# State space scan tiles regrouped: 16 states by 8 channels, with dt and dt·u repeated by DMA

## The reference

```
x = layernorm(x + attention(x))            # 32 heads of 8, relative bias, softmax, wo
x = layernorm(x + ssm(ctx_1024, z=x))      # state space layer, below
x = layernorm(x + moe(x))                  # softmax router, top 1 of 4 experts, silu(g)*u
```

```
dt_low, B, C = split(x_proj(u))            # 8, 16 and 16 rows
dt = softplus(dt_proj(dt_low) + bias)      # per channel d
A = -exp(A_log)                            # 256 channels x 16 states
state[d, n] = state[d, n] * exp(dt[d] * A[d, n]) + dt[d] * u[d] * B[n]   # over tokens
y[d] = sum_n state[d, n] * C[n] + D[d] * u[d];   out = y * silu(z)
```

## Time and profile before

| | us |
|---|---|
| median of the runs | 476.77 |
| the profiled execution, its own time | 477.8 |
| its span (first to last instruction) | 476.0 |
| PE busy | 421.8 (89%) |
| DVE busy | 314.9 (66%) |
| POOL busy | 223.6 (47%) |
| ACT busy | 211.2 (44%) |
| chain that ended last, by engine | PE 63%, DVE 19%, POOL 7%, issue 7%, ACT 2%, DMA 1% |

### The profile page before, as it was taken

The page is one execution under the profiler, slowest core; times in us unless marked ns, Lnnn a source line. Parts: engine busy times, 40 slices in busy tenths (PEclk is TensorE's granted clock), DMA queues, the critical chain, the costliest instruction groups (busy, mean ns, idle before and its releaser), DMA issues.

```text
span 476.0 us, 7872 instructions
## 1 busy us (share of the span) xinstructions
PE 421.8 (89%) x2569; PEld 212.5 (45%) x2570; DVE 314.9 (66%) x626; ACT 211.2 (44%) x412; POOL 223.6 (47%) x246
## 2 busy tenths in 40 slices
PE   5989698878788998989989899986999999999993
PEld 3444223323334443444434444353546666666652
DVE  3598667999988878878889687578314433333444
ACT  2557437566545557745577466712022111111220
POOL 2000518787787569976699768800461111111001
PEclk9999766999989999999999999999999999999997
DMA  9789947717157191674414530069220000000000
GB/s 237 102 269 102 304 138 100 130 64 138 45 117 129 46 154 46 140 195 157 150 72 178 179 98 14 1 251 355 85 61 11 12 4 8 11 11 11 11 1 9
DMA packets 39366, 49.36 MB, mean 104 GB/s; under 512 B 4664, under 2 KB 32673, under 8 KB 39334
## 3 DMA queue, kind: packets, MB, share of 16 engines
q1 hardware_dynamic: 36322, 46.65, 38.8%
q0 software_dynamic: 1056, 2.10, 1.5%
q10 hardware_dynamic: 1956, 0.21, 0.4%
HBM read 40.72 MB, written 8.91 MB: 104 GB/s over the span
## 4 chain that ended last, share of the span: by engine, by line
PE 63%; DVE 19%; POOL 7%; issue 7%; ACT 2%; DMA 1%; POOLq 0%; SPq 0%; DVEq 0%; ACTq 0%
PE ps L1180 16%; PE ps L1196 8%; PE ps L881 7%; PE ps L908 5%; DVE arena L1566 5%; PE ps L912 4%; PE ps L954 4%; DVE arena L1499 4%; PE ps L781 3%; DVE arena L1517 3%; POOL arena L653 2%; PE ps L941 2%; PE ps L1188 2%; POOL arena L659 2%; PE ps L794 2%
## 5 line engine op out<-in xcount | busy, mean ns | idle before, releaser
L1366 ACT ACTIVATE arena<-ps 128x512 f32<-128x512 f32 x128 | 76.2, 595 | 90.7 <-PE ps L941 90.5
L1517 DVE TENSOR_REDUCE arena<-ps 128x2 f32<-128x512 f32 x128 | 86.3, 681 | 27.0 <-PE ps L912 23.0
L659 POOL TENSOR_TENSOR arena<-arena 128x512 f32<-128x512 f32 x60 | 76.2, 1270 | 41.6 <-DVE arena L1566 41.5
L653 POOL TENSOR_TENSOR arena<-arena 128x512 f32<-128x512 f32 x64 | 87.0, 1361 | 4.1 <-issue 3.9
L1180 PE MATMUL ps<-arena 128*128 x176 | 77.5, 593 | 0.7 <-ACT arena L1407 0.7
L1566 DVE TENSOR_TENSOR_SCAN arena<-ps,arena 128x512 f32<-128x512 f32 x60 | 72.8, 1214 | 0.5 <-DVE mv L1611 0.2
L881 PE MATMUL ps<-arena,identf 128*128 128x512 f32 x128 | 68.6, 623 | 0.0
L908 PE MATMUL ps<-arena 48*128 48x256 bf16 x256 | 52.1, 285 | 16.1 <-DVE arena L1517 10.9
L1325 ACT ACTIVATE ps<-arena 128x255 f32<-128x255 f32 x128 | 60.4, 473 | 2.4 <-DVEq L1723 2.4
L1834 DVE TENSOR_TENSOR arena<-arena,ps 128x1024 f32<-128x1024 f32 x11 | 13.4, 1222 | 59.8 <-ACT arena L1411 59.8
L729 POOL DMA_INDIRECT out<-rows_s,arena x11 | 10.8, 985 | 88.7 <-DVE rows_s L1863 80.5
(11 more groups left out here) (231 smaller groups left out, 530.5 us busy)
## 6 DMA issues: line engine op xcount, KB each, us to landing
arena<-bc_d SPq DMA_DIRECT2D x32, 512.0 KB, 4.4
arena<-in_L_ffn_Wg SPq DMA_DIRECT2D x8, 512.0 KB, 5.8
arena<-in_L_ffn_Wu SPq DMA_DIRECT2D x8, 512.0 KB, 6.0
arena<-in_L_ffn_Wd SPq DMA_DIRECT2D x4, 1024.0 KB, 11.8
arena<-kp_d SPq DMA_DIRECT2D x8, 384.0 KB, 8.2
arena<-qp_d SPq DMA_DIRECT2D x8, 384.0 KB, 10.4
qp_d<-arena SPq DMA_DIRECT2D x4, 384.0 KB, 8.6
kp_d<-arena SPq DMA_DIRECT2D x4, 384.0 KB, 8.5
```

What stands on the lines that cost most here:

```text
L653: g.tensor_tensor(dBu[m % 3], dtu[:, :, b * SEQ:(b + 1) * SEQ], over_k(bcr[c % BC_RING][:, m % 2, 0, :]), ALU.mult).then_inc(dbu_ready, 1)
L659: g.tensor_tensor(h, h, over_k(bcr[m // 2 % BC_RING][:, m % 2, 1, :]), ALU.mult).then_inc(hc_ready, 1)
L1366: A(prob[2 * (slot % 2) + kt][:, pr * HALF:(pr + 1) * HALF], ps[:, 2 + n % 2, :], ACT.Exp).then_inc(p_ready, 1)
L1517: v.tensor_reduce(negm[b % 2][:, qt, 2 * pair:2 * pair + 2], ps[:, bank, :].rearrange("p (h k) -> p h k", h=2), axis=AX.X, op=ALU.max).the ...
```

## The change

A tile becomes 16 states by 8 channels, for both halves: partition 8 n + c holds state n of channel c of the group `tile_of(m)`. The 16 tiles of a batch are now 16 groups of 8 channels.

- dt and dt·u of a batch are stored to DRAM (`store_dd`, two stores of 256 KB) and, for each tile, 8 partitions of 4 KB are loaded 16 times over (`load_dd`, 512 KB, a ring of four). ScalarE and GpSimd read this tile. B and C need one load of 256 KB a batch (`load_bc`).
- A is laid out anew (`rates`): transposed by TensorE, exponentiated, stored to DRAM and loaded again by ScalarE's own DMA queue, negated.
- `sum_states(b, q)` sums four tiles at once: `pick` (128 x 32) has ones where partition 8 n + c belongs to column 8 q + c, and each of the four matmuls writes another 32 PSUM partitions.
- `softplus(1)` moves ahead of the loop; the chores begin at n = 3 and come after every unit. `keep_warm(9)` goes. `put_max(0, 1)` comes after the release of the loop. `rows_s` lends its memory to `hst`, `bcs`, `pick` and `rates`, and is set to zero after the loop. `hst` has 8 buffers.

```diff
-BC_RING = 4
-H_RING = 6
+DD_RING = 4
+H_RING = 8
+GROUP = P // STATES
+LANES = 32
...
+        def tile_of(m):
+            n = m % STATES
+            return n % 4 * 4 + n // 4
...
+            def store_dd(b):
+                cols = slice(b * SEQ, (b + 1) * SEQ)
+                sp.wait_ge(dt_ready, b + 1)
+                sp.dma_start(dd_d[b, :, :, 0, :], dts[:, :, cols]).then_inc(dd_out[b], 16)
+                sp.wait_ge(dtu_ready, b + 1)
+                sp.dma_start(dd_d[b, :, :, 1, :], dtu[:, :, cols]).then_inc(dd_out[b], 16)
+            def load_dd(m):
+                b = m // STATES
+                if m % STATES == 0:
+                    sp.wait_ge(dd_out[b], 32)
+                if m >= DD_RING:
+                    sp.wait_ge(da_ready, 2 * (m - DD_RING) + 2)
+                    sp.wait_ge(dbu_ready, m - DD_RING + 1)
+                sp.dma_start(ddr[m % DD_RING],
+                             bass.AP(tensor=dd_d.tensor, offset=(b * P + GROUP * tile_of(m)) * KT * 2 * SEQ,
+                                     ap=[[0, STATES], [KT * 2 * SEQ, GROUP], [1, KT * 2 * SEQ]])
+                             ).then_inc(dd_in[m % DD_RING], 16)
...
             store_parts(1)
             sp.wait_ge(pe_fill, FILL["v3"] + 1)
-            for c in range(BC_EARLY, BC_RING):
-                load_bc(c)
-            for e in range(2):
-                send_max(0, e)
+            load_bc(0)
+            send_max(0, 0)
+            store_dd(0)
+            for m in range(DD_RING):
+                load_dd(m)
+            send_max(0, 1)
             store_bc(1)
             set_ones(1)
+            load_bc(1)
             for h in range(2):
                 load_stack(1, h)
...
-                if slot + BC_RING < QUADS * BATCH:
-                    load_bc(slot + BC_RING)
+                if slot in (1, 4, 7):
+                    store_dd(1 + slot // 3)
+                if b and qd == 1 and b + 1 < BATCH:
+                    load_bc(b + 1)
+                for m in (2 * slot + DD_RING, 2 * slot + DD_RING + 1):
+                    if m < STATES * BATCH:
+                        load_dd(m)
...
-            pool.wait_ge(pe_fill, FILL["v3"] + 1)
-            link(g.memset(rows_s[:, :, :], 0.0))
...
-                g.tensor_tensor(dBu[m % 3], dtu[:, :, b * SEQ:(b + 1) * SEQ], over_k(bcr[c % BC_RING][:, m % 2, 0, :]),
-                                ALU.mult).then_inc(dbu_ready, 1)
+                g.tensor_tensor(dBu[m % 3], ddr[m % DD_RING][:, :, 1, :], over_k(bcs[b % 2][:, 0, :]), ALU.mult).then_inc(dbu_ready, 1)
...
+            pool.wait_ge(y_added, STATES * BATCH)
+            link(g.memset(rows_s[:, :, :], 0.0))
...
-                mm(ps[:, 7, :], identf[:, :], hst[m % H_RING].rearrange("p k l -> p (k l)"), start=(n == 0),
-                   stop=(n == STATES - 1)).then_inc(y_added, 1)
+                for j in range(4):
+                    mm(ps[LANES * j:LANES * (j + 1), 7, :], pick[:, q, :],
+                       hst[(first + j) % H_RING].rearrange("p k l -> p (k l)"), start=(q == 0), stop=(q == 3),
+                       skip_group_check=True).then_inc(y_added, 1)
...
-            keep_warm(9)
...
-                            for late in sums_at(m):
-                                sum_states(late)
+                            if m >= 6 and m % 4 == 2:
+                                sum_states((m - 6) // STATES, (m - 6) % STATES // 4)
...
+            A(rates_n, filled("dtw")[0:STATES, DM:2 * DM].rearrange("p (r d) -> p d r", d=GROUP), ACT.Exp).then_inc(a_exp, 1)
             take("dtw", dtwT, lambda bank: bank[0:RANK, 0:DM])
+            act.wait_ge(a_exp, 1)
+            act.dma_start(rates_d, rates_n.rearrange("p d r -> p (d r)")).then_inc(rates_out, 16)
...
             take("c1", ctxT[:, half(1)])
+            act.wait_ge(rates_out, 16)
+            act.dma_start(rates, rates_d.rearrange("n (d r) -> (n d) r", d=GROUP)).then_inc(rates_in, 16)
...
-                A(dA[m % 2][:, k, 1:SEQ], dts[:, k, b * SEQ + 1:(b + 1) * SEQ], ACT.Exp,
-                  scale=acol[:, k, n:n + 1]).then_inc(da_ready, 1)
+                A(dA[m % 2][:, k, 1:SEQ], ddr[m % DD_RING][:, k, 0, 1:SEQ], ACT.Exp,
+                  scale=rates[:, at:at + 1]).then_inc(da_ready, 1)
...
-                if n % 2 and chores:
+                if n >= 3 and chores:
                     chores.pop(0)()
-            put_max(0, 1)
...
             dve.sem_inc(scan_in, 1)
+            put_max(0, 1)
...
-                        elif m < SOFT_STEPS * (BATCH - 1):
-                            softplus(1 + m // SOFT_STEPS, m % SOFT_STEPS)
+                        elif m < SOFT_STEPS * (BATCH - 2):
+                            softplus(2 + m // SOFT_STEPS, m % SOFT_STEPS)
```

More of the change, by code:

```diff
@@ L192, in decoder_layer @@
         assert sq_at + HALF * len(squares) <= top[0]
+        squares_1 = [arena[:, tiles_at + HALF * i:tiles_at + HALF * (i + 1)].rearrange("p (k l) -> p k l", k=KT)
+                     for i in range(len(LOG1P_ROOTS))]
         u = carve(KT * TOK, KT, TOK)
@@ L254, in decoder_layer @@
         rows_s = sb("rows_s", [P, SLOTS, DM])
+        spare = rows_s[:, :, :].rearrange("p s d -> p (s d)")
+        hst += [spare[:, HALF * i:HALF * (i + 1)].rearrange("p (k l) -> p k l", k=KT) for i in range(2)]
+        bcs = [spare[:, 2 * HALF + HALF * i:2 * HALF + HALF * (i + 1)].rearrange("p (i l) -> p i l", i=2) for i in range(2)]
+        at = 4 * HALF
+        pick = spare[:, at:at + P].rearrange("p (q c) -> p q c", c=LANES)
+        rates = spare[:, at + P:at + P + KT * P // GROUP]
+        rates_n = spare[0:STATES, at + 2 * P:at + 2 * P + KT * P].rearrange("p (d r) -> p d r", d=GROUP)
+        each_d = spare[:, at + 2 * P + KT * P:at + 2 * P + KT * P + GROUP]
         wT = rows_s[:, 0:3 * KT, :]
@@ L279, in decoder_layer @@
         bc_out = [sem(f"bc_out{h}") for h in range(2)]
-        bc_in = [sem(f"bc_in{i}") for i in range(BC_RING)]
+        bc_in = [sem(f"bc_in{i}") for i in range(2)]
+        dd_out = [sem(f"dd_out{b}") for b in range(BATCH)]
+        dd_in = [sem(f"dd_in{i}") for i in range(DD_RING)]
+        pick_ready = sem("pick_ready")
+        rates_out = sem("rates_out")
+        rates_in = sem("rates_in")
+        rates_ready = sem("rates_ready")
         y_out = sem("y_out")
@@ L837, in _ @@
             for k in range(KT):
-                last = nc.tensor.transpose(ps[0:RANK, bank, k * P:(k + 1) * P], dtw[:, k, :], identf[:, :])
+                nc.tensor.transpose(ps[0:RANK, bank, k * P:(k + 1) * P], dtw[:, k, :], identf[:, :])
+            for k in range(KT):
+                last = nc.tensor.transpose(ps[0:STATES, bank, DM + k * P:DM + (k + 1) * P], alog[:, k, :], identf[:, :])
             filled(last)
@@ L1314, in _ @@
                 A(yT[:, k, :], u[:, k, :], ACT.Copy, scale=dcol[:, k:k + 1]).then_inc(yt_set, 1)
-            for step in range(SOFT_STEPS):
-                square(step)
+            for b in range(2):
+                for i in range(len(LOG1P_ROOTS)):
+                    square(b, i)
             take("low1", xdbl[:, half(1)], lambda bank: bank[0:XR, :])
@@ L1331, in _ @@
                 decay(0, k)
+            late_square(0)
             def copy_context(n):
@@ L1459, in _ @@
             v.tensor_copy(diag[:, SPREAD:SPREAD + 1], diag[:, 0:1]).then_inc(diag_ready, 1)
+            link(v.memset(pick, 0.0))
+            dve.wait_ge(consts, 1)
+            link(v.tensor_reduce(each_d, identf[:, :].rearrange("p (n d) -> p d n", d=GROUP), axis=AX.X, op=ALU.add))
+            for q in range(4):
+                link(v.tensor_copy(pick[:, q, GROUP * q:GROUP * (q + 1)], each_d))
+            dve.sem_inc(pick_ready, 1)
             def leave(n, hf):
@@ L1706, in _ @@
             chores = [lambda k=k: put_u(k, 1) for k in range(KT)] + \
-                     [lambda step=step: softplus(0, step) for step in range(SOFT_STEPS)]
+                     [lambda b=b, step=step: softplus(b, step) for b in range(2) for step in range(SOFT_STEPS)]
             for n, unit in enumerate(A_UNITS[0, -1]):
@@ L1711, in _ @@
                     put_max(0, 0)
-                if n % 2 and chores:
+                if n >= 3 and chores:
                     chores.pop(0)()
-            put_max(0, 1)
-            while chores:
-                chores.pop(0)()
             for name in ("v3", "low1", "dt01"):
@@ L1723, in _ @@
             dve.sem_inc(scan_in, 1)
+            put_max(0, 1)
+            assert not chores
             for b in range(BATCH):
```

103 lines of the change are left out of this document (47 added, 56 removed).

## The result

| | before | after |
|---|---|---|
| median in the comparison (4 runs each), us | 476.58 | 486.75 |
| ratio | | 1.0221 [1.0153, 1.0289] |
| span of the profiled execution, us | 476.0 | 484.4 |
| mean granted clock of TensorE | 0.966 | 0.895 |

The change makes the kernel slower by 2.2% (1.5 to 2.9%), where 458.4 us were forecast. The page of the changed kernel: the chain that ended last by engine and by line, SyncE's queue, and two DMA issues (names, count, KB each, us to landing).

The account below looks back on a forecast made before the run. TensorE was taken to bound batches 1 to 3, VectorE batch 0. From the median of 476.8 us: start +2.0, queue +4.1, softplus -5.5, batches -5, -6, -6, end -2, in all -18.4, so 458.4 us; range 446 to 472.

Parts of the forecast that it names:

- TensorE's sums: Sums over states in the loop: a group of four takes 1.05 us, so TensorE loses 11.5 us a batch.
- What a batch gets back: Loop, batches 1 to 3: 5, 6 and 6 us shorter, with VectorE's busy time over 0.95 as next bound.
- Softplus: Batch 0: five of 15 softplus steps leave the loop, saving 1.1 us a tile, 5.5 us in all.
- the release sees little: Ahead of the loop: four moved softplus steps, 3.4 us of work, hardly delay the release of the loop.
- The start: Before scan 0: dt's trip through DRAM, the rates' store and smaller effects add 2.0 us, from -1 to +6.
- The DMA queue: Batch 0: tiles 4 and 5 wait behind batch 1's four stack loads, +4.1 us, from 0 to 8.
- just held: Later stack loads in SyncE's queue: each adds up to 6.2 us ahead of a tile, only some 3 us stay.
- The first sign that I had named for being wrong: Loop: the prediction is wrong if waits for the tile loads recur in batches 1 to 3.
- The end: After scan 63: one group replaces sums 61, 62 and 63, -2 us, from 0 to -4.
- The tiles come late: Rival, 8%: the DMA queue bounds the loop, nine more late loads at 3 us each, 485.4 us.
- The next engine is nearer: Rival, 15%: in the loop VectorE and GpSimd take over at once when the sums go, 469.4 us.
- A lower clock: Rival, 4%: TensorE idles at batch 0's two waits and its clock falls, 463 us.

Follow-up runs that it names:

- after_no_tile_loads: The changed kernel without its 64 tile loads, ScalarE and GpSimd reading dt and dt·u in place (result not the reference's): 471.08 us, ratio 0.9850.
- before_thin_sums: The kernel before with each of the 64 sums over states cut from 512 to 128 columns, no other edit: 473.68 us, ratio 0.9933.
- before_soft: The kernel before with softplus(1) moved ahead of the loop and chores from n = 3 after every unit, full output: 474.77 us, ratio 0.9964.
- thin_half_weigh: The kernel before with 128-column sums, loop stacks on ScalarE's queue, useless TensorE products, and GpSimd's row C product for half the channels: 464.30 us, ratio 0.9723.

## Why the prediction failed, by its steps

By parts, forecast and then measured between the profiled executions (us): start +2.0 and +3.5, batch 0 -1.4 and -0.6, batch 1 -5 and +7.8, batch 2 -6 and +0.5, batch 3 -6 and -2.6, end -2 and -0.1; in all -18.4 and +8.4. Of the 22.6 us missed in batches 1 to 3, 6.8 go with the tile loads (after_no_tile_loads) and 15.8 stay.

- **TensorE's sums**: right. A group takes 0.99 to 1.06 us (1.05 forecast) and they overlap.
- **What a batch gets back**: the step that failed. I priced batches 1 to 3 at -17 us, with VectorE's busy time over 0.95 as the floor. before_thin_sums makes it -5.7 in the batches and -3.3 in the median; with the stacks in another queue and the clock at 0.98 to 1.00, -8.2. The 95% came from batch 0, where VectorE has softplus steps that wait for no scores. In batches 1 to 3 its maxima alternate with `scores_a`, and in the kernels with thin sums and whole maxima VectorE was busy 82 to 87% of batches 1 and 2, whatever else was cut. The row that pointed there was in my hands: 7.3 us of VectorE's idle behind L912, which I counted as slack to be had. I also took the 10.5 us of L881 in the chain for nearly all that the 16 sums take, while my own price for them was 15.7: in a third of their time something else was on the chain already. Without its tile loads the changed kernel is still 1.7 and 2.8 us above before_thin_sums in batches 1 and 2; that part stays open.
- **Softplus**: right in mechanism, short in size: 7.0 us in before_soft against 5.5. What the move costs ahead of the loop, which I took for nothing ("the release sees little"), was 4.7 us there, with the nine `keep_warm` products (2.59 us in the chain) in the same stretch.
- **The start**: +2.0 forecast, +3.5 measured. The trip of dt through DRAM was not the last wait; GpSimd stood until the release at 76.4 us. What moved the release was ScalarE's wait for the rates, for which I had 1.8 us: its store took 6.91 us to land, not 4.5, and the products behind the pause took 5.78 instead of 3.72 us (the clock is 0.61 from 26 to 33 us; in the kernel before it is 1.00 from 24 to 31 us). Moving that wait returned 3.8 us.
- **The DMA queue**: the second step that failed, and the one that makes the change slower: +4.1 us forecast, 13.2 measured by taking the loads away. The place of the first late load was right, its price was not. Scans 0 to 4 take 7.2 us more than before; I had 4.1 (its upper bound was 8). The other stack loads, of which I wrote "just held", did not hold: tile 20 landed 11.46 us after its issue, not 4.4 and 3 more. Without the loads batch 1 is 6.4 us shorter. The first sign that I had named for being wrong, waits for tile loads in batches 1 to 3, is in the chain of all three. The stores and tile loads queued ahead of the stacks stood in my sum only as a share of the engines' time, not as a delay.
- **The end**: nothing, not -2: scan 63 to the last `put_y` takes 7.3 us in both.
- **Rivals**: "The tiles come late" named the outcome (485.4) with 8%; that its number is 1.3 us off the measured one is luck. It kept the whole gain of the sums and added nine late loads at 3 us; in fact most of that gain was never there, and the chain has five waits for tiles, of which those in batches 2 and 3 cost 0.1 and 0.3 us. "The next engine is nearer" (469.4, 15%) had the mechanism that holds without the loads (471.08), though with GpSimd in it, which thin_half_weigh clears. "A lower clock" was seen (0.966 to 0.895); raising it again gained nothing in the whole.
